# Gated cross attention and a sparse gated FFN on one core: GpSimd's share of the work rearranged, the down weights split anew each time, a new last step

## The reference, cut to what matters

```python
x = x + tanh(g_xattn) * xattn(layernorm(x), ctx, mask)      # x, ctx: (32, 128, 512), float32
#   scores = x @ ctx.T / sqrt(512), masked, softmax, @ ctx; zero where no memory is valid
x = x + tanh(g_ffn) * ffn(layernorm(x), w_gate, w_up, w_down)
#   h = silu(x @ w_gate) * (x @ w_up)                        # (..., 2048)
#   h: of every 4 neighbours the 2 of largest magnitude stay, the others are 0
#   out = h @ w_down                                         # (..., 512)
```

## Time and profile before

| | |
|---|---|
| median of 3 runs | 1163.98 us (1161.43 to 1169.27) |
| the profiled execution | 1164.87 us, of it 1163.1 us span |
| PE busy | 1091.0 us, 94% |
| DVE busy | 790.7 us, 68% |
| ACT busy | 605.8 us, 52% |
| POOL busy | 230.7 us, 20% |
| mean granted TensorE clock | 0.982 of full speed |
| HBM read, written | 168.82 MB, 114.29 MB |

### The profile page before, as it was taken

One profiled execution on the slowest core, in us unless ns is written; L12 is line 12 of the kernel. 1 busy time (PEld: TensorE's weight loads), 2 busy tenths in 40 slices (PEclk: granted clock), 3 DMA queues, 4 the chain that ended last, 5 costly groups with the idle time before them and its releaser, 6 DMA issues.

```text
span 1163.1 us, 15073 instructions
## 1 busy us (share of the span) xinstructions
PE 1091.0 (94%) x4960; PEld 888.9 (76%) x4960; DVE 790.7 (68%) x1365; ACT 605.8 (52%) x1092; POOL 230.7 (20%) x413
## 2 busy tenths in 40 slices
PE   6988888799998999999999999999999999999967
PEld 5766566587776878888888788888888888888846
DVE  6999847969697676666675667575847373747480
ACT  6988556567675444444444445444544344444432
POOL 5767300313122131111110011011011111111112
PEclk9999898999999999999999999999999999999989
DMA  7999586798989997788789877887888766778445
GB/s 261 349 382 340 189 285 222 290 344 270 323 251 296 370 304 191 190 237 257 192 261 299 279 195 199 228 270 199 270 274 255 159 161 152 230 158 221 94 109 72
DMA packets 94078, 279.92 MB, mean 241 GB/s; under 512 B 9200, under 2 KB 9200, under 8 KB 89072
## 3 DMA queue, kind: packets, MB, share of 16 engines
q1 hardware_dynamic: 75568, 245.40, 59.3%
q0 software_dynamic: 18432, 33.56, 21.6%
HBM read 168.82 MB, written 114.29 MB: 243 GB/s over the span
## 4 chain that ended last, share of the span: by engine, by line
PE 70%; DVE 13%; DMA 9%; issue 3%; ACT 3%; SPq 1%; POOL 1%; POOLq 0%; ACTq 0%; DVEq 0%
PE ps_y L1086 9%; PE ps_y L1088 9%; PE ps_y L1087 9%; PE ps_a L1017 8%; PE ps_a L1021 8%; PE ps_a L1019 8%; PE ps_d L1017 4%; PE ps_d L1019 4%; PE ps_d L1021 4%; DMA x_blk<-xnT_scratch 3%; PE ps_c L1021 2%; PE ps_c L1017 2%; PE ps_c L1019 2%; DMA w_raw<-in_L_ffn_w_up 2%; DVE beats L849 2%
## 5 line engine op out<-in xcount | busy, mean ns | idle before, releaser
L536 POOL DMA_DIRECT2D out_rows<-y_out x128 | 110.7, 865 | 768.9 <-ACT y_out L640 741.5
L1086 PE MATMUL ps_y<-dn,h_hi 128*128 128x512 f32 x512 | 203.6, 398 | 24.6 <-DMA dn<-dn_scratch 11.4
L1017 PE MATMUL ps_a<-xm,w_ring 128*128 128x512 f32 x512 | 203.2, 397 | 15.3 <-DVE w_ring L277 7.3
L1019 PE MATMUL ps_a<-xm,w_ring 128*128 128x512 f32 x512 | 202.4, 395 | 0.0
L1021 PE MATMUL ps_a<-xm,w_ring 128*128 128x512 f32 x512 | 202.4, 395 | 0.0
L1088 PE MATMUL ps_y<-dn,h_lo 128*128 128x512 f32 x512 | 202.0, 395 | 0.0
L1087 PE MATMUL ps_y<-dn,h_hi 128*128 128x512 f32 x512 | 201.7, 394 | 0.0
L640 ACT ACTIVATE y_out<-ps_y,ffn_gate 128x512 f32<-128x512 f32 x128 | 88.0, 688 | 199.4 <-PE ps_y L1088 199.4
L817 DVE TENSOR_TENSOR cp<-ps_c,cp 128x512 f32<-128x512 f32 x64 | 43.9, 691 | 150.7 <-PE ps_c L1021 150.7
L1086 PEld LDWEIGHTS ps_y<-dn,h_hi 128*128 128x128 f32 x512 | 97.5, 190 | 49.0 <-DMA dn<-dn_scratch 11.8
L1017 PEld LDWEIGHTS ps_a<-xm,w_ring 128*128 128x128 f32 x512 | 97.6, 191 | 38.1 <-issue 9.5
(11 more groups left out here) (91 smaller groups left out, 1750.5 us busy)
## 6 DMA issues: line engine op xcount, KB each, us to landing
w_ring<-w_scratch SPq DMA_DIRECT2D x147, 512.0 KB, 4.6
out_rows<-y_out POOLq DMA_DIRECT2D x128, 256.0 KB, 4.1
w_scratch<-w_ring SPq DMA_DIRECT2D x56, 512.0 KB, 8.1
xm_scratch<-x_out SPq DMA_DIRECT2D x42, 512.0 KB, 5.2
xm<-xm_scratch SPq DMA_DIRECT2D x21, 1024.0 KB, 7.0
dn<-dn_scratch SPq DMA_DIRECT2D x9, 2048.0 KB, 11.1
x_in<-in_x SPq DMA_DIRECT2D x32, 256.0 KB, 6.3
ctx_in<-in_ctx SPq DMA_DIRECT2D x32, 256.0 KB, 6.4
```

Source lines behind the costliest of these rows:

```text
L536: nc.gpsimd.dma_start(out[RING * ((s - 1) // QS) + TILES * ORDER[order] + n % TILES], y_out[:, n % 4], accum_op=ALU.add).then_inc(y_stored ...
L1017: nc.tensor.matmul(to, w_ring[:, k, e, 0, c], xm[:, k, 0, c], start=begins and c == 0, stop=False, skip_group_check=not begins)
L1019: nc.tensor.matmul(to, w_ring[:, k, e, 0, c], xm[:, k, 1, c], start=False, stop=False, skip_group_check=not begins)
L1086: nc.tensor.matmul(to, h_hi[:, h, j, at], dn[:, 0, j], start=at_j == 0, stop=False)
```

## The change

- **Attention, inputs:** the rings of x and ctx have 10 places instead of 8; all 10 are loaded before the first raw weights, and batch n+5 is loaded in slot n (before n+3).
- **Attention, statistics:** DVE takes the first norm's statistics of batch n+1 in slot n, with a slot -1 ahead. GpSimd's three powers become one on up to three columns (`base3`, `exponent3`, `power3`), the two epsilon adds one.
- **Attention, low parts:** the 7 w_low of unit 0 and the 14 x_low of pair 0 are done by GpSimd, not DVE, at the end of its slot.
- **FFN, building:** the w_low of k = 4 to 6 of an odd unit come after DVE's two add_c11 of that unit.
- **Down weights:** the DRAM copy is made quarter by quarter. Nothing is stored or reloaded; in the 13 steps of `DN_BUILT` the quarter is loaded raw (from step 5 on into the free w_raw buffer, ahead of time), and split by ACT and GpSimd. ACT's four dn_high stand between the copies of a1, ahead of x_high and copy_d0.
- **Last step:** its down weights have a place of their own (`dn_last`, over xm), magnitudes of its second half go to x_blk instead of over h_hi, h_high moves ahead among the copy_y, and the last four tiles are added by DVE to rows loaded from DRAM, and stored by SP.

```diff
-DN_RELOADED = [s for s in range(QS, STEPS) if s % QS]
+LAST = STEPS - 1
+DN_BUILT = [s for s in range(STEPS) if s < QS or s % QS]
...
+        def dn_places(s, j):
+            if s < QS:
+                return dn[:, 1, j].bitcast(F32), dn[:, 0, j], dn[:, 1, j]
+            to = dn_last if s == LAST else dn
+            return w_raw[:, j // 2, j % 2], to[:, 0, j], to[:, 1, j]
+
+        def abs_of(s, order):
+            return x_blk if (s, order) == (LAST, 1) else h_abs[:, ORDER[order]]
...
+            def copy_down(q):
+                sp.dma_start(raw_dram[q], down_view[q]).then_inc(down_copied, 16)
+
             def load_dn(s):
-                wait(sp, y_done, 2 * TILES * s)
                 if s < QS:
-                    if s == 0:
-                        sp.wait_ge(down_copied, 16)
-                    else:
-                        sp.wait_ge(dn_stored, 16 * s)
+                    wait(sp, y_done, 2 * TILES * s)
+                    wait(sp, dn_lo_done, GROUP * s)
+                    sp.wait_ge(down_copied, 16 * (s + 1))
                     sp.dma_start(dn[:, 1]..., raw_dram[s]).then_inc(dn_raw_loaded, 16)
                 else:
-                    if s == DN_RELOADED[0]:
-                        sp.wait_ge(dn_stored, 16 * QS)
-                    sp.dma_start(dn[:]..., dn_dram[weights_of(2 * s) // 2]).then_inc(dn_loaded, 16)
+                    sp.wait_ge(spread_done, 4 * BUILT)
+                    sp.wait_ge(dn_lo_done, GROUP * DN_BUILT.index(s))
+                    sp.dma_start(w_raw[:]..., down_view[weights_of(2 * s) // 2]).then_inc(dn_raw_loaded, 16)
...
-            for b in range(RING):
+            for b in range(INPUTS):
                 load(b)
...
-                    if n + 3 < B:
-                        load(n + 3)
+                    if n + 5 < B:
+                        load(n + 5)
...
-                        if half == 0 and s > 0:
-                            store_dn(s - 1)
+                        if half == 0:
+                            if s + 1 < QS:
+                                sp.wait_ge(down_copied, 16 * (s + 1))
+                                copy_down(s + 1)
...
+            sp.wait_ge(made[2], 2 * UNITS)
+            for t in range(TILES):
+                n = TILES * (2 * LAST - 1) + t
+                sp.wait_ge(y_stored[n % 4], 16 * (n // 4 + 1))
+            b = B - RING + TILES * ORDER[1]
+            sp.dma_start(rows[:], out.rearrange("b s d -> s b d")[:, b:b + TILES]).then_inc(rows_loaded, 16)
+            for t in range(TILES):
+                sp.wait_ge(y_added, t + 1)
+                sp.dma_start(out[b + t], rows[:, t]).then_inc(rows_stored, 16)
...
         @block.gpsimd
+            for n in range(-1, SLOTS - 1):
+                k = n % RING
+                first, second, third = n + 1 < B, 0 <= n - 6 < B, 0 <= n - 4 < B
+                if first:
+                    pool.wait_ge(stats1_done, n + 2)
+                if second:
+                    pool.wait_ge(stats2_done, n - 5)
+                if first or second:
+                    part_v = slice(0 if first else 1, 2 if second else 1)
+                    nc.gpsimd.tensor_tensor(base3[:, k, part_v], bn_mv[:, k, part_v, 1], eps[:, part_v], ALU.add)
+                    pool.wait_ge(base_done, n + 2)
+                if first:
+                    nc.gpsimd.tensor_tensor(neg_mean[:, k:k + 1], bn_mv[:, k, 0, 0:1], minus_one[:], ALU.mult)
+                if third:
+                    pool.wait_ge(probs_done, n - 3)
+                part_p = slice(0 if first else 1, 3 if third else 2 if second else 1)
+                nc.gpsimd.tensor_tensor(power3[:, k, part_p], base3[:, k, part_p], exponent3[:, part_p], ALU.pow)
...
+                if n - 1 in W0_AT:
+                    w_low(pool, nc.gpsimd, 0, W0_AT[n - 1])
+                if n - 1 in X0_AT:
+                    x_low(pool, nc.gpsimd, 0, *X0_AT[n - 1])
...
+            for s in range(STEPS):
+                if s in DN_BUILT and s != LAST:
+                    dn_low(s)
+                for t in range(TILES):
+                    add_y(2 * TILES * s + t)
+                if s == LAST - 1:
+                    dn_low(LAST)
+                if s != LAST:
+                    for t in range(TILES, 2 * TILES):
+                        add_y(2 * TILES * s + t)
...
         @block.scalar
                 silu0(u, 0)
                 silu0(u, 1)
+                if s - 1 in DN_BUILT:
+                    dn_high(s - 1, 0)
                 copy_a1(u, 0)
+                if s - 1 in DN_BUILT:
+                    dn_high(s - 1, 1)
                 copy_a1(u, 1)
+                if s - 1 in DN_BUILT:
+                    dn_high(s - 1, 2)
+                    dn_high(s - 1, 3)
                 x_high_at(s, 0)
...
-                if 0 < s <= QS:
-                    for j in range(GROUP):
-                        dn_high(s - 1, j)
...
+                if s == LAST:
+                    for j in range(GROUP):
+                        absolute(s, 1, j)
+                    for t, tiles in enumerate(((), kept_order(s)[:1], kept_order(s)[1:], ())):
+                        copy_y(s - 1, 1, t)
+                        for j in tiles:
+                            h_high(s, 0, j)
+                    break
...
         @block.vector
-                    for k in range(2, PROD):
+                    for k in range(2, 4):
                         w_low(dve, nc.vector, u + 1, k)
...
                 add_c11(u, 0)
                 add_c11(u, 1)
+                if u < BUILT:
+                    for k in range(4, PROD):
+                        w_low(dve, nc.vector, u, k)
...
-            s = STEPS - 1
+            s = LAST
+            compare(s, 1, ((0, 1), (2, 3)))
             for j in kept_order(s):
                 h_low(s, 0, j)
-            compare(s, 1, ((0, 1),) + REST + ((2, 3),))
+            compare(s, 1, REST)
             count_wins(s, 1)
             keep(s, 1, kept_order(s))
             for j in kept_order(s):
                 h_low(s, 1, j)
+            for t in range(TILES):
+                n = TILES * (2 * LAST + 1) + t
+                dve.wait_ge(y_done, n + 1)
+                if t == 0:
+                    dve.wait_ge(rows_loaded, 16)
+                nc.vector.scalar_tensor_tensor(rows[:, t], ps_y[n % 2][:], ffn_gate[:], rows[:, t], ALU.mult, ALU.add)
```

More of the change, by code:

```diff
@@ L32 @@
 RING = 8
+INPUTS = 10
 LAG = 7
@@ L497, in _ @@
[L497 to L505 removed]
+            pool.wait_ge(half_done, 2)
+            pool.wait_ge(base_set, 1)
@@ L716, in _ @@
                 copy_a1(u, 1)
+                if s == LAST:
+                    for j in range(GROUP):
+                        dn_high(s, j)
                 x_high_at(s, 2)
@@ L975, in _ @@
                 h_low(s, 1, j)
+            for t in range(TILES):
[3 more added lines that the diff above has]
+                    dve.wait_ge(rows_loaded, 16)
+                nc.vector.scalar_tensor_tensor(rows[:, t], ps_y[n % 2][:], ffn_gate[:], rows[:, t], ALU.mult,
+                                               ALU.add).then_inc(y_added, 1)
         @block.tensor
@@ L1057, in _ @@
                     wait(pe, x1_done, b - 1)
-                    nc.tensor.matmul(ps_av[b % 2][:], probsT[:, b % 2], ctx_in[:, b % RING], start=True,
+                    nc.tensor.matmul(ps_av[b % 2][:], probsT[:, b % 2], ctx_in[:, b % INPUTS], start=True,
                                      stop=True).then_inc(av_done, 1)
@@ L1071, in down @@
                 h = ORDER[order]
-                if s < QS:
-                    pe.wait_ge(dn_lo_done, GROUP * (s + 1))
-                elif s in DN_RELOADED:
-                    pe.wait_ge(dn_loaded, 16 * (DN_RELOADED.index(s) + 1))
+                if s in DN_BUILT:
+                    pe.wait_ge(dn_lo_done, GROUP * (DN_BUILT.index(s) + 1))
+                right = dn_last if s == LAST else dn
                 for t in range(TILES):
                     n = TILES * hs + t
-                    wait(pe, y_copied, n - 1)
+                    if (s, order) == (LAST, 1) and t >= 2:
+                        pe.wait_ge(y_added, t - 1)
+                    else:
+                        wait(pe, y_copied, n - 1)
                     if n < 2:
@@ L1085, in down @@
                             pe.wait_ge(h_lo_done, kept_count(s, order, j))
[L1086 to L1088 removed]
+                        nc.tensor.matmul(to, h_hi[:, h, j, at], right[:, 0, j], start=at_j == 0, stop=False)
+                        nc.tensor.matmul(to, h_hi[:, h, j, at], right[:, 1, j], start=False, stop=False)
+                        last = nc.tensor.matmul(to, h_lo[:, h, j, at], right[:, 0, j], start=False, stop=at_j == GROUP - 1)
                     last.then_inc(y_done, 1)
```

202 lines of the change are left out of this document (93 added, 109 removed).

## The result

The changed kernel takes 1161.78 us (median of 12 runs, 1158.37 to 1162.74) against 1165.47 (12 runs) for the kernel before: ratio 0.9965, 95% interval 0.9951 to 0.9979. It moved 4 us where the sum of the prediction had 13. The profiled execution is the quickest of its runs (1158.37 us, span 1156.6), 3.4 us under their median; before, the span was 1163.1, and that execution lay 0.6 under its median.

The account below looks back on a forecast made before the run. TensorE, busy 94% of the span, was taken as the bound, with gains only in attention, building steps and end. Terms -14.8 - 6 + 2.7 - 0.7 + 0 + 0.8 + 5 = -13.0 led to 1151 us, range 1138 to 1164.

Parts of the forecast that it names:

- The end: Last step: shorter wait for down weights, last 96 matmuls at full clock, shorter path behind them; -14.8 us.
- The start: Before the attention: four more input loads, 1.05 MB, ahead of the first raw weights delay ACT; +2.7 us.
- Attention: Attention slots: DVE loses 21 subtractions, part lost again to GpSimd's lock; merged powers end no bounding wait; -6 us.
- The low parts' term: Attention slots 13 to 35: 17 subtractions off DVE, 10.2 us, less 4.5 lost beside sums; -5.7 us.
- Full steps: Nine steps from step 4: GpSimd's subtractions delay DVE's comparisons and the add before product 6; +5, between 0 and 8.4.
- the full price: Full steps: four locks at 1.0 us per step, less slack, make TensorE wait 0.4 to 1.6 each; 8.4 us.
- Building steps: Four building steps: TensorE's waits for GpSimd's low part vanish, but DVE sets the end; 0 us.
- step 1: Building step 1: raw quarter lands late, ACT stops 3.4 us and TensorE's k = 4 waits behind copy_a1; +0.8 us.
- Behind the attention: After the attention: ACT waits for the last normed rows' store, then a DRAM copy of 1 MB, not 4; -0.7 us.
- signs of being wrong: TensorE losing more than 10 us between 460 and 1060 us, or the attention ending later than before.
- the whole-length lock: Full steps: each of 36 subtractions stops DVE for 1.30 us, 19.3 instead of 5; 1165 us, chance 0.1.
- The third rival: Only the end pays; attention gives nothing, as ACT, TensorE or DMA queues bound its slots too; 1157 us, chance 0.15.

Follow-up runs that it names:

- experiment 5: Four separate attention edits, each on the changed kernel with rounded copies behind copy_d0; the one giving the second norm its own base sum and power: 1146.01 us.
- experiment 3: The changed kernel's feed-forward part and end with the whole attention of the kernel before: 1161.03 us, ratio 0.9967.
- experiment 6: The changed kernel with ScalarE's four rounded copies behind both copies of a1, still ahead of copy_d0: 1157.87 us, ratio 0.9944.

## Why the prediction was wrong

The total of 1151 missed by 11 us, though 1161.8 lay inside the range. What failed is the gain: 13 us were forecast and 3.7 came, 6.5 in the pair of profiles and 2.8 less by their distance from the medians. Two terms carry the miss: the attention at -6, which gave 1.5, and the full steps at +5, which took 8.5. By its steps:

- **The end**, -14.8: right, 15.4 in the pair, partly by luck: the wait gave 10.3 (10.6 forecast), the 96 last matmuls 2.4 (3.4) and the path behind them 2.7 (0.8), because the plain store landed in 2.0 us where 4.1 had been put. The end alone gave 13 us (interval 10 to 17).
- **The start**, +2.7: right in mechanism, low by a little. Slot 6 came 3.6 us later in the pair, and with the raw weights first it came about 3 us sooner.
- **Attention**, -6: the step that failed is the sentence that the merged powers "by themselves end no wait that bounds a slot", with "DVE's 1.3 us between statistics and second norm" as cover. The low parts' term was good (5.7 forecast between slots 13 and 35, 5.5 measured over the 28 slots). But GpSimd's path from the aggregate to the power's end was costed by its load, which shrinks, and not by its length, which grows: base, neg_mean and a power of 0.85 us (0.589 for one column) in series end at 83.91 in the slot shown, 1.5 us behind the start of the aggregate. VectorE's own work in between is done at 83.73, and the second norm begins at 84.02, a wait of 0.29. A slot without low part or sum became 0.37 us longer, and went back when the power was split (experiment 5). Net of other gains this cost 3.9 us of 28 slots. The prediction named the cover and its size, and did not add up the chain against it. It also took 3.14 us for the floor of a slot from a mean that holds one slot with a low part (the others are 3.04), and left out the wait in slot 30, though the earlier trace rows has its 2.3 us on VectorE; that the attention gained at all in the pair is due to that slot, and no term of the sum foresaw it.
- **Full steps**, +5: a term mis-sized. The mechanism, the place (ahead of product 6) and the single waits were right: for steps 4, 8, 10, 11, 12, 14 and 15 the full price was put at 1.0, 1.0, 1.0, 1.6, 0.4, 0.4 and 0.4; measured were 1.61, 1.63, 1.61, 2.23, 1.03, 1.02 and 1.02, each 0.6 more. What failed was the halving between 0 and the full price of 8.4. One GpSimd operation in an attention slot that found no turn was no measure of how often four subtractions would; seven of nine steps paid in the changed kernel's trace, nine of nine in experiment 3's and six of nine in experiment 6's. The full price would also have been low, 8.4 for nine steps against waits of 10.1 in seven or 14.0 in nine: four subtractions cost the comparisons 4.4 us, 1.10 each, not 1.0, which is 0.4 of the 0.6.
- **Building steps**, 0, **and step 1**, +0.8: -0.8 in the pair. ScalarE's wait in step 1 was 3.37 us (3.4 forecast), and TensorE lost 0.2 by it, not 0.8; that the later quarters would not be waited for was wrong (3.96 and 3.31), but TensorE's waits in those two steps sum to 8.7 us where they had been 8.4.
- **Behind the attention**, -0.7: -0.9 in the pair.

One of the prediction's own signs of being wrong came: the attention ended later than before (143.85 against 141.77). The other did not in this trace (7.5 us lost between 460 and 1060 us; 11.4 in experiment 3's). Of the rivals, the whole-length lock came nearest in time (1165), but not by its reason: a subtraction cost a comparison 1.10 us, between the 1.0 of the forecast and the 1.30 of that rule, and in up to three steps of nine nothing at all. The third rival, that the attention gives nothing and only the end pays (1157), named the outcome, though with another cause. The Trainium skill ("SBUF — State Buffer", section "SBUF: two separate sides") lets the first to start keep the ports for an instruction while the other fully blocks. That the two engines take turns in a stretched step agrees with it: in step 8 the first comparison, begun 0.37 us into a subtraction of 1.61, took 1.79 instead of 0.69; that GpSimd gets no turn through a whole run of comparisons in others (in experiment 6's step 7 the first one took 5.15 us) is more than it states. The chances had 0.55 on faster by over 1% and 0.37 on within 1%, which is what came.

## What to carry to other kernels

When tiny operations are merged, compare the length of the chain from the last input to the first user with the cover, not the engine's load: the merged operation runs longer than one of its parts (0.85 us here against 0.55), and every user waits for all of it. Price the parts of a change apart, by kind of slot: here a loss of 0.4 us in most slots hid behind one slot's gain of 3. A lock between two engines cost 10 us or nothing here, by what stood behind it on the queue; put the operation that collides beside work that nobody waits for, and where that can't be, budget the full price for every occurrence.

## What was not expected of the hardware

- A GpSimd power on three columns takes 0.85 us, on two 0.70, on one 0.55 to 0.59, while its additions and products take 0.19 on one column and 0.20 on two (0.48 for the one that begins beside VectorE's second norm, at 84.13 in the slot above).
- Beside four GpSimd subtractions of 128x512, six VectorE comparisons of 128x512 from SBUF took either 8.1 us or 3.7, with nothing between, at offsets between the two engines that agree within 0.01 us (experiment 6). In the second case GpSimd's four took 7.8 to 10.4 us instead of 6.5 to 7.0.
- Beside a GpSimd subtraction of 128x512, VectorE's statistics (bn_stats, 0.68 us) and operations with an input in PSUM (0.69 and 0.74 us) were not stretched. Those with both large inputs in SBUF were, and so was the second norm, which has one such input and two values per partition: 0.55 us alone, 1.41 to 1.55 in the one slot of nine traces in which a low part is under way when it begins.

```profile
140.48 1.54 DVE L859 TENSOR_SCALAR x1n<-x,bn_mv,power 128x512 f32<-128x512 f32 x1 [0.53 <-POOL power L532]
...
140.45 1.29 POOL L332 TENSOR_TENSOR xm<-x_blk,xm 128x512 fp32r<-128x512 f32 x1
```
